# Moving one expert group, half of the values and the first norm's statistics within a unit, with a second norm and a key spread in other operations

## The reference

```python
x = x + conv(_ln_c(x), w_qkv, b_qkv, w_proj, b_proj, rel_table)   # norm over channels, eps 1e-6
t = to_tokens(x)
t = t + ffn(_ln_t(t), gate_w, gate_b, w1, b1, w2, b2)             # norm over channels, eps 1e-5

# conv: windows of 7 x 7 on the image rolled by -4, and back by 3, 12 heads of 8 channels
attn = einsum('bhwnqd,bhwnkd->bhwnqk', q, k) / sqrt(8) + bias + mask
o = einsum('bhwnqk,bhwnkd->bhwnqd', softmax(attn), v)
return roll_back(o) @ w_proj.T + b_proj

# ffn: 4 experts with 384 hidden units, the two best of them count
probs = softmax(x @ gate_w + gate_b)
masked = probs * mask_of_top_2(probs)
masked = masked / (sum(masked) + 1e-9)
h = gelu(x @ w1[e] + b1[e]);  y = h @ w2[e] + b2[e]
return sum_e masked[e] * y[e]
```

## Time and profile before

| | us |
|---|---|
| median of 3 runs | 7628.7 (7628.25 to 7630.38) |
| the profiled execution | 7625.72 |
| its span, first to last instruction | 7623.5 |

### The profile page before, as it was taken

One profiled execution on the slowest core, in us unless ns is written; L12 is line 12 of the kernel. 1 busy time (PEld: TensorE's weight loads), 2 busy tenths in 40 slices (PEclk: granted clock), 3 DMA queues, 4 the chain that ended last, 5 costly groups with the idle time before them and its releaser, 6 DMA issues.

```text
span 7623.5 us, 237214 instructions
## 1 busy us (share of the span) xinstructions
PE 7145.0 (94%) x88320; PEld 5850.0 (77%) x88320; DVE 5436.6 (71%) x17442; ACT 4162.8 (55%) x8191; POOL 1481.6 (19%) x777
## 2 busy tenths in 40 slices
PE   6999999999999999999999999999999999999998
PEld 4777777777777777778777777777777777777777
DVE  6777777777777777777777777777777777777775
ACT  3555555555555555555555555555555555555554
POOL 2112111221112111211121112211221112111211
PEclk9999999999999999999999999999999999999999
DMA  1111111111111111111111111111111111111110
GB/s 48 34 32 34 32 33 31 34 33 33 31 33 34 33 31 33 33 32 33 32 34 32 34 31 35 32 33 31 33 34 33 31 33 34 34 31 32 34 33 18
DMA packets 168186, 250.49 MB, mean 33 GB/s; under 512 B 44514, under 2 KB 129122, under 8 KB 166882
## 3 DMA queue, kind: packets, MB, share of 16 engines
q1 hardware_dynamic: 167010, 234.60, 11.0%
HBM read 80.28 MB, written 38.54 MB: 16 GB/s over the span
## 4 chain that ended last, share of the span: by engine, by line
PE 81%; DVE 9%; issue 5%; POOL 2%; ACT 1%; SPq 1%; DVEq 0%; POOLq 0%; DMA 0%
PE ps_f L1026 24%; PE ps_t L938 10%; PE ps_o L955 8%; PE ps_f L866 8%; PE ps_f L867 7%; PE ps_f L868 7%; PE ps_s L918 5%; PE ps_s L928 4%; POOL rstd L410 2%; DVE stat L623 2%; PE ps_f L1023 2%; DVE stat L696 1%; DVE xr L693 1%; ACT pt_sb L500 1%; PE ps_f L874 1%
## 5 line engine op out<-in xcount | busy, mean ns | idle before, releaser
L1026 PE MATMUL ps_f<-w_sb,g_sb 128*112 128x96 f32 x18432 | 1961.7, 261 | 0.0
L1026 PEld LDWEIGHTS ps_f<-w_sb,g_sb 128*112 128x112 f32 x18432 | 1918.8, 178 | 0.0
L500 ACT ACTIVATE pt_sb<-ps_t 113x588 f32<-113x588 f32 x1024 | 676.1, 660 | 1939.7 <-PE ps_t L938 1926.7
L484 ACT ACTIVATE g_sb<-ps_f 128x392 f32<-128x392 f32 x3072 | 1523.7, 497 | 374.1 <-PE ps_f L868 350.5
L801 DVE SCALAR_TENSOR_TENSOR xr<-ps_f,gate,xr 112x96 f32<-112x96 f32 x3072 | 787.6, 311 | 989.8 <-PE ps_f L1026 985.4
L410 POOL TENSOR_TENSOR rstd<-ve,cst 112x4 f32<-112x4 f32 (+1 forms) x256 | 269.3, 1052 | 5478.3 <-DVE ve L705 5478.3
L866 PE MATMUL ps_f<-x_hi,w_hi 128*128 128x392 f16 x3072 | 1086.6, 354 | 107.4 <-issue 101.4
L867 PE MATMUL ps_f<-x_lo,w_hi 128*128 128x392 f16 x3072 | 1083.1, 353 | 0.0
L868 PE MATMUL ps_f<-x_hi,w_lo 128*128 128x392 f16 x3072 | 1077.2, 351 | 0.0
L665 DVE TENSOR_REDUCE s_max<-ps_s 113x12 f32<-113x588 f32 x1024 | 783.3, 765 | 355.5 <-PE ps_s L928 326.5
L938 PE MATMUL ps_t<-ident,p_sb 113*113 113x113 f32 x6144 | 854.7, 275 | 3.6
(11 more groups left out here) (117 smaller groups left out, 10160.1 us busy)
## 6 DMA issues: line engine op xcount, KB each, us to landing
k_st<-qk_hi SPq DMA_DIRECT2D x768, 49.0 KB, 1.9
q_st<-qk_hi SPq DMA_DIRECT2D x768, 49.0 KB, 2.0
xr<-x SPq DMA_DIRECT2D x224, 139.1 KB
out<-xr SPq DMA_DIRECT2D x224, 139.1 KB
xa<-x SPq DMA_DIRECT2D x224, 136.5 KB
k_st<-qk_lo SPq DMA_DIRECT2D x384, 49.0 KB, 1.9
q_st<-qk_lo SPq DMA_DIRECT2D x384, 49.0 KB, 2.0
xa<-x SPq DMA_DIRECT2D x224, 10.5 KB
```

Source lines behind the costliest of these rows:

```text
L484: nc.scalar.activation(g_sb[:, chunk, half * STRIP:(half + 1) * STRIP], h_bank[k % 3][:, 0:STRIP], ACT.Gelu, scale=1.0 / WSCALE).then_inc( ...
L1026: ins = T.matmul(y[:, k * C:(k + 1) * C], g_sb[:, e * CPE + c, j * LANES:(j + 1) * LANES], w2_sb[:, e * CPE + c, :], start=False, stop=(c ...
```

## The change

Five things are edited.

- Expert group 7 leaves iteration 6 and stands behind `attend(a, 7)`. Its combine on VectorE moves from the last iteration to between `qk_low(b, 1)` and `qk_low(b, 2)`.
- `values(b)` is split: the first bank stands behind `turn_o(a, 7)`, the second behind expert group 8.
- `ln1_stats` leaves the unit's end and stands in the next step, behind `spread_keys`, for the same unit.
- The second norm is no longer a centring and a scaling of four and of three tiles, but one operation per tile with two per-row operands, and TensorE waits for each tile.
- `spread_keys` has four operations over all three groups instead of twelve. In the router two scalar_tensor_tensor operations become a tensor_scalar and a tensor_tensor each.

```diff
--- before.py
+++ after.py
@@ -102,7 +102,7 @@
 
 TURNS = [(2 * b + s, e) for b in range(3) for e in range(EXPERTS) for s in range(2)]
 TURNS = [TURNS[3 * g:3 * g + 3] for g in range(8)] + [[(W - 1, e) for e in range(EXPERTS)]]
-GROUPS_AT = ((0, 1), (2,), (3,), (4,), (5,), (6,), (7,), (), ())
+GROUPS_AT = ((0, 1), (2,), (3,), (4,), (5,), (6,), (), ())
 
 
 T1_AT = 4
@@ -120,7 +120,7 @@
 N_XHI, N_X1LO = 4, 4
 N_COMB = 7 * EXPERTS
 N_STACK = 16 * 3 * GROUPS
-N_KBD = GROUPS * GH
+N_KBD = GH
 QSCALE = HD ** -0.5
 QK_SCALE = (QSCALE / WSCALE, 1.0 / WSCALE)
 
@@ -248,13 +248,13 @@
         rec_done = sem("rec_done")
         res_done = sem("res_done")
         stat2_done, aggr2_done, var2_done = sem("stat2_done"), sem("aggr2_done"), sem("var2_done")
-        rstd2_done, centre2_done = sem("rstd2_done"), sem("centre2_done")
+        rstd2_done = sem("rstd2_done")
         norm2_done, x2lo_done = sem("norm2_done"), sem("x2lo_done")
         gate_ready = sem("gate_ready")
         router = sem("router")
         comb_done = sem("comb_done")
 
-        N_ROUTER = 13
+        N_ROUTER = 15
 
         def windows(t):
             return t.rearrange("p (h w c r) -> p h w c r", h=2, w=NW, c=W)
@@ -654,10 +654,9 @@
             def spread_keys(a):
 
                 dve.wait_ge(k_in, at(a, N_STACK, N_STACK))
-                for g in range(GROUPS):
-                    for j in range(GH):
-                        V.tensor_scalar(k_bd[0:C, g, j, :], k_st[:, g, :], head_rows[:, j:j + 1], None,
-                                        ALU.mult).then_inc(kbd_done, 1)
+                for j in range(GH):
+                    V.tensor_scalar(k_bd[0:C, :, j, :], k_st[:, :, :], head_rows[:, j:j + 1], None,
+                                    ALU.mult).then_inc(kbd_done, 1)
 
             def softmax_pair(a, n):
                 scores = ps_s[0:SPAN, 0:HEADS * NB].rearrange("p (h k) -> p h k", k=NB)[:, :, 0:WW]
@@ -705,27 +704,19 @@
                     V.tensor_scalar(ve2[:, j0:j0 + n], mv2[:, j0:j0 + n, 1], EPS_T, None, ALU.add
                                     ).then_inc(var2_done, 1)
 
-                def centre(k, j0, n):
-                    V.tensor_tensor(xn2[:, j0:j0 + n, :], rows[:, j0:j0 + n, :],
-                                    mv2[:, j0:j0 + n, 0:1].broadcast_to([LANES, n, C]), ALU.subtract
-                                    ).then_inc(centre2_done, 1)
-
                 def scale(k, j0, n):
-                    dve.wait_ge(centre2_done, at(f, 2, k + 1))
                     dve.wait_ge(rstd2_done, at(f, 2, k + 1))
-                    V.tensor_tensor(xn2[:, j0:j0 + n, :], xn2[:, j0:j0 + n, :],
-                                    rstd2[:, j0:j0 + n].unsqueeze(2).broadcast_to([LANES, n, C]),
-                                    ALU.mult).then_inc(norm2_done, 1)
+                    for t in range(j0, j0 + n):
+                        V.tensor_scalar(xn2[:, t, :], rows[:, t, :], mv2[:, t, 0:1], rstd2[:, t:t + 1],
+                                        ALU.subtract, ALU.mult).then_inc(norm2_done, 1)
 
                 dve.wait_ge(xr_in[u], f[0] * per + (f[1] // UPI + 1) * per)
                 first_part, second_part = (0, 0, 4), (1, 4, 3)
                 sums_of(*first_part)
                 variances(*first_part)
                 sums_of(*second_part)
-                centre(*first_part)
                 variances(*second_part)
                 scale(*first_part)
-                centre(*second_part)
                 scale(*second_part)
                 x2_low(f, 0)
                 x2_low(f, 1)
@@ -771,15 +762,16 @@
                                      ALU.mult))
                 link(V.tensor_tensor(ggt[:, :, :], ggt[:, :, :], geq[:, :, :], ALU.add))
                 link(V.tensor_reduce(rank[:, :], ggt[:, :, :], AX.X, ALU.add))
-                link(V.scalar_tensor_tensor(out=gsel[:, :, :].rearrange("p t e -> p (t e)"), in0=rank[:, :],
-                                            scalar=1.5, in1=ge.rearrange("p t e -> p (t e)"),
-                                            op0=ALU.is_lt, op1=ALU.mult))
                 V.tensor_reduce(gtot[:, :], ge, AX.X, ALU.add).then_inc(router, 1)
                 k[0] += 1
+                link(V.tensor_scalar(rank[:, :], rank[:, :], 1.5, None, ALU.is_lt))
+                link(V.tensor_tensor(gsel[:, :, :].rearrange("p t e -> p (t e)"), rank[:, :],
+                                     ge.rearrange("p t e -> p (t e)"), ALU.mult))
+                V.tensor_scalar(gtot[:, :], gtot[:, :], 1e-9, None, ALU.mult).then_inc(router, 1)
+                k[0] += 1
                 link(V.tensor_reduce(gden[:, :], gsel[:, :, :], AX.X, ALU.add))
 
-                link(V.scalar_tensor_tensor(out=gden[:, :], in0=gtot[:, :], scalar=1e-9, in1=gden[:, :],
-                                            op0=ALU.mult, op1=ALU.add))
+                link(V.tensor_tensor(gden[:, :], gden[:, :], gtot[:, :], ALU.add))
                 link(V.reciprocal(gden[:, :], gden[:, :]))
                 assert k[0] == N_ROUTER
                 V.tensor_tensor(gate[:, :].rearrange("p (t e) -> p t e", e=EXPERTS), gsel[:, :, :],
@@ -816,7 +808,7 @@
             def attention(a, b, f=None, u=None):
 
                 for n in range(8):
-                    if f is not None and n:
+                    if f is not None and 0 < n < 7:
                         combine(f, u, n)
                     if n < 7:
                         softmax_pair(a, n + 1)
@@ -831,9 +823,9 @@
                 normalise_o(a, 7)
                 if b is not None:
                     qk_low(b, 1)
-                    c = following(b)
-                    if c is not None:
-                        ln1_stats(c)
+                if f is not None:
+                    combine(f, u, 7)
+                if b is not None:
                     qk_low(b, 2)
                 residual(a)
                 if b is not None:
@@ -846,6 +838,8 @@
             def step(f, a, b, u):
                 if a is not None:
                     spread_keys(a)
+                    if b is not None:
+                        ln1_stats(b)
                 router_b(f)
                 if a is not None:
                     softmax_pair(a, 0)
@@ -976,8 +970,8 @@
                 for k, (j0, n) in enumerate(((0, 4), (4, 3))):
                     if k == 1 and b is not None:
                         qk(b, 3)
-                    pe.wait_ge(norm2_done, at(f, 2, k + 1))
                     for j in range(n):
+                        pe.wait_ge(norm2_done, at(f, W, j0 + j + 1))
                         ins = T.transpose(bank[5 + k][0:C, j * LANES:(j + 1) * LANES], xn2[:, j0 + j, :],
                                           ident[0:LANES, 0:LANES])
                     ins.then_inc(t2_done, 1)
@@ -1065,14 +1059,17 @@
                 if b is not None:
                     qk(b, 1)
                 attend(a, 7)
-                if b is not None:
-                    values(b)
+                if f is not None:
+                    experts(f, 7)
                 turn_o(a, 7)
                 if b is not None:
+                    values(b, (0,))
                     qk(b, 2)
                 project(a)
                 if f is not None:
                     experts(f, 8)
+                if b is not None:
+                    values(b, (1,))
                 transpose2(a, b)
                 hidden(a, (0, 1))
                 gate_scores(a)
```

## The result

The changed kernel takes 8064.6 us (median of 4 runs, 8061.91 to 8067.02) against 7628.5 of the kernel before on the same chip (4 runs, 7625.63 to 7630.38): a ratio of 1.057, interval 1.0554 to 1.059. It is 436 us slower. The forecast was 8140 in a range of 7820 to 8210. The profiled execution has a span of 8060.1 us, so its loss against the span of before is 436.6.

A forecast was written before the change was run, and what follows sets the result against it. TensorE, busy 94%, was taken to bound the kernel, losing time at the unit's end. 94 x (1.35 + 2.7 + 0.8) plus 30 x (1.35 + 0.5) gave 512 us more, about 8140; range 7820 to 8210.

The forecast's parts named there:

- The unit's end, +1.35: Last stretch of each unit: ScalarE copies the late second half of the values first, so the hidden layer starts 1.35 us later.
- the upper bound that I had given: Cost of the unit's end if the projection's wait does not shrink: +1.6 us per unit.
- The second norm, nothing: VectorE at the unit's end: one operation per token could bring transposes 0.3 us earlier, but ScalarE's chain covers it; nothing booked.
- The spread, 5.25: Key spread on VectorE at the step's head: four operations over 2352 columns take 5.25 us, 1.05 more than before.
- half the rate: Key spread: assumed middle step between keeping four columns a nanosecond and falling to one.
- The statistics and the router, 1.96 and 5.0: VectorE's head: moved statistics take 1.96 us, the router 5.0, its selection and denominator sum held by GpSimd's centring and scaling.
- the rival that said otherwise: Router at the head: tensor_tensor is not held by GpSimd, router takes some 2.95 us, total 7870; chance 0.17.
- The head as a whole, 12.2 and 2.7 late: Step's head on VectorE: spread, statistics and router sum to 12.2 us, costing 2.7 us per ordinary unit before TensorE's second scores.
- The second drop of the clock, 0.8 in each ordinary unit: TensorE's stall before the second scores brings another clock drop, 1.1 us in three units of four, 0.8 on average.
- The drop at the unit's end I leave as it is.: TensorE's existing clock drop around the hidden layer's start, 1.1 us lost per unit, was taken as unchanged.
- Units behind the branch, +1.85: The 30 units after the loop's branch: 1.35 us more at the end and 0.5 at the head.
- One bound of the forecast: Lower end of the forecast's own spread, 7990 us: no second clock drop and the unit's end at +0.9.

The follow-up runs named there:

- the padded rows: The changed kernel with two unused columns behind each row of the stacked keys, so the spread's source and destination both have three rows: 7948.3 us, ratio 1.0421.

## Why the prediction was right

The sign, the order of the parts and the mechanism of the end and of the head were right; what the clock does was not, and the sum of 512 came out 75 too high for it. Term by term, in its order:

- **The unit's end, +1.35.** From the transposes of iteration 6 to the hidden layer a unit took 4031.87 - 4014.45 = 17.42 us; in the unit of the earlier trace rows this stretch was 15.82. That is +1.60, and the upper bound that I had given was 1.6. Of the 0.25 missed, 0.18 lies ahead of the projection. The chain on ScalarE is the one worked out, with the same starts: the second copies idle until the values, load, copy, low part. The residual starts 1.21 behind the projection; I had it 1.26 behind.
- **The second norm, nothing.** Right under the chain. The experiments put it at 0.14 per unit where nothing covers it; I had said 0.3 and more.
- **The spread, 5.25.** 5.39 from its start to that of the statistics. The value was right, and the reason too: the padded rows show that it is the shape that costs. From the rows of before alone it was partly luck: they had no such form, and "half the rate" was only the step between two ends.
- **The statistics and the router, 1.96 and 5.0.** 1.95 and 4.98. The two holds came where they were placed: tensor_tensor is held (median 1216 and 1110 ns over the run), so the rival that said otherwise fell.
- **The head as a whole, 12.2 and 2.7 late.** 12.32, and gmax to softmax grew by 2.87 in the median and 2.63 in the mean. TensorE's own wait for it, which I had put at 2 to 3 us, is 1.2, for the reason two points down.
- **The second drop of the clock, 0.8 in each ordinary unit.** Mis-sized. I had three units in four at 1.1 us each. Low clock is in the attention of 28 of 119 units, 0.80 us of it on average, which at half speed is 0.4 us lost per unit: a drop is rarer than I said, and costs 1.7 us where it comes.
- **"The drop at the unit's end I leave as it is."** This is the step that failed. In the earlier trace rows the drop lay on the products that the gate waits for. With a longer stall in another place most of it lies behind them (on these products the low clock fell from 1.92 to 0.64 us per unit): hidden to gmax is 1.74 instead of 2.71 in the median, 1.79 instead of 2.61 in the mean, a gain of 0.8. There it slows products that TensorE works on while VectorE's late head runs anyway. Instead of two drops on the path, a unit mostly has one, and that one hidden: 3.4 us at half speed eat 1.7 us of the stall, which is then 0.94 and not 2.63 and rarely followed by another. The run with the values whole, which has no drop there, shows the 2.63.
- **Units behind the branch, +1.85.** They came to 2.3 in the mean, of which the end alone gives 2.0.

Made anew with the measured sizes, by the means: 1.60 for the end, 2.63 for the head, -0.82 for the drop that moved, 0.4 for those in the attention, is 3.8 for an ordinary unit, as measured. One bound of the forecast does not come out of its own terms: without a second drop and with the end at +0.9 the sum is 94 x 3.6 + 30 x 1.4 = 380, which gives 8009 and not 7990.

The parts do not add up when made alone: 198 (group and values), -36 (statistics), 0 (router), 194 (spread over the statistics) and -20 (norm) are 336 of the 436. The rest is not taken apart by a run of its own. Two things point at it: behind a late head the new router is no longer free (the gate is done at 14.35, and at 13.92 with the old router, which is held twice as well), and the statistics' own gain at the end does not exist while ScalarE's chain lies over it; their move costs 224 us with the rest of the change in place, and alone it brings 36. What stays open is by what the place of a drop is set within the unit. The runs show the drops behind stalls, and that with one stall shortened the drop came behind the next; they don't give a rule by which I could have placed it beforehand.

## What to carry to other kernels

Before you move work away from a place, price what it leaves behind as carefully as where it goes: the same statistics cost nothing in the middle of the attention, 0.5 us and a drop of the clock at the unit's end, about 1 us at a head that has 0.8 to spare, and 2 us at one that the spread has made late already (59.38 to 61.46). Price a stall of TensorE together with the drop of the clock behind it and ask what that drop lies on, since it can cost 1.7 us or nothing; here taking one stall away paid in full only where no other stood ready to take the drop over. A tensor_scalar, tensor_tensor or scalar_tensor_tensor on VectorE with its operands in SBUF that meets GpSimd's centring or scaling costs the rest of that operation's 1.3 us, while a reduction does not, so time the release of GpSimd's work, and don't make fewer and larger operations of many without looking at how their rows divide.
